# Local projections of a transformer block: q and k as fp32r products, rows turned a tile earlier, q and k rotated together

## The reference

```python
DIM, DEPTH, HEADS, DIM_HEAD, WINDOW, INNER = 256, 2, 8, 64, 128, 512
def _layer(x, wqkv, qs, ksc, wo, ...):
    b, n, _ = x.shape
    h = shift_token(x)              # second half of the features comes from the token before
    qkv = h @ wqkv                  # 256 -> 3 x 512
    q, k, v = jnp.split(qkv, 3, axis=-1)
    q, k, v = (to_heads(q), to_heads(k), to_heads(v))
    q = l2norm(q) * qs
    k = l2norm(k) * ksc
    q, k = rotary_xpos(q, k)        # q*cos*scale + rotate_half(q)*sin*scale; k likewise with 1/scale
    o = local_attention(q, k, v)    # windows of 128, each with the one before
    x = x + o @ wo
    ...
```

## Time and profile before

| | |
|---|---|
| median of 3 runs | 2562.07 us (2554.25 to 2565.87) |
| the profiled execution | 2577.46 us |
| its span, first to last instruction | 2575.8 us |
| busy: TensorE | 2240.0 us (87%) |
| busy: VectorE | 1242.6 us (48%) |
| busy: ScalarE | 1043.7 us (41%) |
| busy: GpSimd | 691.2 us (27%) |
| mean granted TensorE clock | 0.946 |
| first stage of local projections | from 542.5 to 674.6 us |
| second stage | from 937.3 to 1067.9 us |

### The profile page before, as it was taken

The page is one execution under the profiler, slowest core; times in us unless marked ns, Lnnn a source line. Parts: engine busy times, 40 slices in busy tenths (PEclk is TensorE's granted clock), DMA queues, the critical chain, the costliest instruction groups (busy, mean ns, idle before and its releaser), DMA issues. The chain is left out here.

```text
span 2575.8 us, 43116 instructions
## 1 busy us (share of the span) xinstructions
PE 2240.0 (87%) x13642; PEld 1649.2 (64%) x13643; DVE 1242.6 (48%) x2758; ACT 1043.7 (41%) x2555; POOL 691.2 (27%) x684
## 2 busy tenths in 40 slices
PE   7997497769897999898998989799998489879998
PEld 4664497534565864466875654479997256557887
DVE  4664200479775249876325653000000456567864
ACT  1663132313565433466424652124443046544332
POOL 1000201347422547522531001300001410054443
PEclk8998699889999999999999999899999689999999
DMA  7761242110000000000028622113221376100000
GB/s 190 160 156 69 82 166 83 31 41 0 25 0 16 24 17 0 25 0 15 1 47 146 125 36 86 51 47 128 83 105 46 102 149 128 33 27 25 25 25 33
DMA packets 110695, 164.17 MB, mean 64 GB/s; under 512 B 15258, under 2 KB 95115, under 8 KB 105579
## 3 DMA queue, kind: packets, MB, share of 16 engines
q1 hardware_dynamic: 101570, 140.55, 21.6%
q0 software_dynamic: 7680, 20.98, 2.6%
q10 hardware_dynamic: 1320, 1.03, 0.2%
HBM read 114.83 MB, written 47.32 MB: 63 GB/s over the span
## 5 line engine op out<-in xcount | busy, mean ns | idle before, releaser
L1037 DVE TENSOR_REDUCE xa_mx<-ps 128x2 f32<-128x512 f32 x384 | 246.8, 685 | 98.3 <-PE ps L689 97.2
L141 PE MATMUL ps<-ones 128*128 128x384 f32 (+1 forms) x450 | 163.9, 493 | 100.2 <-DMA ex_rows<-rows_out,rows_back 37.8
L896 ACT ACTIVATE xn_tok<-ps 128x512 f32<-128x512 f32 x384 | 210.5, 602 | 52.6 <-PE ps L697 50.9
L1467 PEld LDWEIGHTS ps<-ex_xT,ex_w 128*128 128x128 f32 x1792 | 211.8, 194 | 7.3 <-issue 4.5
L1467 PE MATMUL ps<-ex_xT,ex_w 128*128 128x128 f32 x1792 | 212.4, 277 | 3.8 <-issue 3.8
L1474 PE MATMUL ps<-ex_w,ex_h 128*128 128x256 f32 x896 | 202.7, 379 | 0.0
L141 PEld LDWEIGHTS ps<-ones 128*128 128x128 f32 x450 | 90.3, 221 | 144.7 <-issue 51.6
L689 PE MATMUL ps<-xa_ks,xa_qs 48*128 48x256 f32 (+1 forms) x768 | 158.5, 324 | 27.0 <-DMA xa_qs<-x_queries 8.9
L1474 PEld LDWEIGHTS ps<-ex_w,ex_h 128*128 128x128 f32 x896 | 165.9, 190 | 20.2
L2128 PE MATMUL ps<-lo_w,lp_hs 128*128 128x512 f32 x384 | 173.6, 603 | 4.7 <-ACT lp_hs L2176 2.8
L689 PEld LDWEIGHTS ps<-xa_ks,xa_qs 48*128 48x128 f32 (+1 forms) x768 | 107.7, 194 | 100.3 <-DVE xa_mx L1037 51.2
(11 more groups left out here) (345 smaller groups left out, 4994.9 us busy)
## 6 DMA issues: line engine op xcount, KB each, us to landing
xa_ks<-x_keys SPq DMA_DIRECT2D x144, 128.0 KB
xa_qs<-x_queries SPq DMA_DIRECT2D x144, 128.0 KB, 4.5
ex_w<-in_L0f_w_dram SPq DMA_DIRECT2D x16, 1024.0 KB, 7.2
ex_w<-in_L2f_w_dram SPq DMA_DIRECT2D x16, 1024.0 KB, 6.8
x_keys<-xa_khl SPq DMA_DIRECT2D x24, 512.0 KB, 5.6
x_queries<-xa_qhl SPq DMA_DIRECT2D x24, 512.0 KB, 3.0
ex_stage<-rows_in POOLq DMA_DIRECT2D x64, 128.0 KB
rows_out<-ex_rows SPq DMA_DIRECT2D x56, 128.0 KB, 1.7
```

The source lines that it names most:

```text
L141: self.nc.tensor.matmul(self.ps[:, bank, 0:wide * P], self.ones[:], self.ones[:].unsqueeze(1).to_broadcast([P, wide, P]), start=True, stop ...
L896: nc.scalar.activation(pT[:, h % SLOTS].rearrange("p k q -> p (k q)"), c.ps[:, S_BANK + (HEADS * b + n) % 3], ACT.Exp).then_inc(exped.sem, 1)
L1037: nc.vector.tensor_reduce(mx[:, half, :, col], c.ps[:, M_BANK + h % 2].rearrange("p (t n) -> p t n", t=2), AX_X, ALU.max).then_inc(max_put ...
L1467: ins = nc.tensor.matmul(c.ps[:, f % 4, 0:P], w1[:, buf, k, f * P:(f + 1) * P], xT[:, k], start=(k == 0), stop=(k == KD - 1))
```

## The change

Four things in `local_projections`, and what goes with them:

- q and k are made of fp32r products. Weights and rows are split into a rounded part (`lead`) and the rest (`less`). A tile's list on TensorE is: rounded rows times rounded weights and times the rests of the weights (8 products), v as before (2 fp32 products), then the rests of the rows times the rounded weights (4 products). ScalarE copies the turned rows twice, first rounded, then whole; GpSimd subtracts (`rest`). At the start of a layer ScalarE rounds the weights of q and k, and VectorE subtracts.
- `turn_rows(i + 1, ...)` stands ahead of `project(i, 1)` in TensorE's loop, with the same wait. On ScalarE the copies of the rows stand ahead of the square.
- VectorE rotates q and k of a tile together, with four operations of twice the size; GpSimd rotates nothing.
- `wo` is loaded at the start of `local_weighing` instead of during the projections; squares and t2 share a buffer; four `keep_busy` products stand behind the first `turn_rows`.

The diff, cut:

```diff
 def rotate
+        def rotate(dve, step, tt):
+            a = t1[:, tt].rearrange("p a (h d) -> p a h d", h=LH)
+            b = t2.rearrange("p a (h d) -> p a h d", h=LH)
             for lo, hi in ((0, HALF), (HALF, LD)):
...
+                step.mark(nc.vector.tensor_tensor(
+                    b[:, :, :, lo:hi], src, tab[:, :, 1, tt, lo:hi].unsqueeze(2).to_broadcast([P, 2, LH, HALF]), ALU.mult))
+            step.settle(dve)
+            step.link(dve, nc.vector.tensor_tensor(
+                a, a, tab[:, :, 0, tt].unsqueeze(2).to_broadcast([P, 2, LH, LD]), ALU.mult))
+            return nc.vector.tensor_tensor(a, a, b, ALU.add)
@@ gpsimd
-            def rotate_k(i, tt):
...
+            def rest(i):
+                pool.wait_ge(*h_put(i + 1))
+                nc.gpsimd.tensor_tensor(hl[:], hs[:], hh[:].bitcast(F32), ALU.subtract).then_inc(h_rest.sem, 1)
             stage(0)
+            rest(0)
             with pool.Fori(0, B - 1) as i:
                 stage(i + 1)
-                rotate_k(i, 0)
-                rotate_k(i, 1)
+                rest(i + 1)
@@ tensor, project(i, tt)
-                pe.wait_ge(*h_put(i + 1))
+                pe.wait_ge(*h_lead(i + 1))
                 pe.wait_ge(*lengthed(2 * i + max(tt - 1, 0)) if tt else lengthed(2 * i - 1))
                 pe.wait_ge(*v_put(2 * i) if tt else v_put(2 * i - 1))
-                for n in range(3):
+                rows = slice(tt * P, (tt + 1) * P)
+                for n in range(2):
+                    pe.wait_ge(*w_rest(n + 1))
+                    for a, wp in enumerate((wh, wl)):
+                        for k in range(KD):
+                            nc.tensor.matmul(c.ps[:, 3 * tt + n, :], hh[:, k, rows], wp[:, k, n * INNER:(n + 1) * INNER],
+                                             start=(a == 0 and k == 0), stop=False)
+                pe.wait_ge(*h_put(i + 1))
+                for k in range(KD):
+                    nc.tensor.matmul(c.ps[:, 3 * tt + 2, :], hs[:, k, rows], wqkv[:, k, 2 * INNER:], start=(k == 0),
+                                     stop=(k == KD - 1))
+                pe.wait_ge(*h_rest(i + 1))
+                for n in range(2):
                     for k in range(KD):
-                        ins = nc.tensor.matmul(c.ps[:, 3 * tt + n, :], hs[:, k, tt * P:(tt + 1) * P],
-                                               wqkv[:, k, n * INNER:(n + 1) * INNER],
-                                               start=(k == 0), stop=(k == KD - 1))
+                        ins = nc.tensor.matmul(c.ps[:, 3 * tt + n, :], hl[:, k, rows], wh[:, k, n * INNER:(n + 1) * INNER],
+                                               start=False, stop=(k == KD - 1))
@@ tensor, the list
             turn_rows(0, h_put(0))
-            pe.wait_ge(*w_in(16))
+            c.keep_busy(4, 0)
+            pe.wait_ge(*pool_s(2))
...
                 project(i, 0)
                 turn_qk(i - 1, 0, i + 1)
+                turn_rows(i + 1, qk_put(4 * i - 2))
                 project(i, 1)
-                turn_rows(i + 1, qk_put(4 * i - 2))
                 turn_qk(i - 1, 1, i + 2)
@@ scalar
-                nc.scalar.copy(hs[:, 0, :], c.ps[:, 6, 0:S])
-                nc.scalar.copy(hs[:, 1, 1:S], c.ps[:, 6, S:2 * S - 1]).then_inc(h_put.sem, 1)
+                for rows, sgn in ((hh, h_lead), (hs, h_put)):
+                    nc.scalar.copy(rows[:, 0, :], c.ps[:, 6, 0:S])
+                    nc.scalar.copy(rows[:, 1, 1:S], c.ps[:, 6, S:2 * S - 1]).then_inc(sgn.sem, 1)
             def take(i, tt, between=None):
                 act.wait_ge(*qkv_done(2 * i + tt + 1))
+                if between is not None:
+                    put_rows(between)
                 act.wait_ge(*summed(2 * i + tt))
                 nc.scalar.activation(sq, ..., ACT.Square).then_inc(squared.sem, 1)
-                if between is not None:
-                    put_rows(between)
...
+            act.wait_ge(*w_in(16))
+            lead_w(0)
             put_rows(0)
+            lead_w(1)
@@ vector
+            for n in range(2):
+                cols = slice(n * INNER, (n + 1) * INNER)
+                dve.wait_ge(*w_lead(n + 1))
+                nc.vector.tensor_tensor(wl[:, :, cols], wqkv[:, :, cols], wh[:, :, cols].bitcast(F32), ALU.subtract
+                                        ).then_inc(w_rest.sem, 1)
@@ local_weighing
+            sp.wait_ge(*loaded(16))
+            sp.dma_start(wo[:], dram["L1f_wo"][d]).then_inc(loaded.sem, 16)
```

More of the change, by code:

```diff
@@ L2063, in local_projections @@
         zst, hs = sb("zst", [P, 2, D]), sb("hs", [P, KD, S])
-        sq, ss = sb("sq", [P, 2 * INNER]), sb("ss", [P, 2, 2 * LH])
+        (wh, wl), (hh, hl) = ([c.sb(f"lp_{n}_{part}", shape, F32R, ctx) for part in ("lead", "less")]
+                              for n, shape in (("w", [P, KD, 2 * INNER]), ("h", [P, KD, S])))
+        w_lead, w_rest, h_lead, h_rest = (c.sig(n) for n in ("w_lead_put", "w_rest_put", "h_lead_put", "h_rest_put"))
+        ss = sb("ss", [P, 2, 2 * LH])
         root, rn = sb("root", [P, 2, 2 * LH]), sb("rn", [P, 2, 2 * LH])
@@ L2073, in _ @@
             fetch(sp)
-        def rotate(engine, eng, step, tt, side):
-            a = t1[:, tt, side].rearrange("p (h d) -> p h d", h=LH)
-            b = t2[:, tt, side].rearrange("p (h d) -> p h d", h=LH)
+        def rotate(dve, step, tt):
+            a = t1[:, tt].rearrange("p a (h d) -> p a h d", h=LH)
+            b = t2.rearrange("p a (h d) -> p a h d", h=LH)
             for lo, hi in ((0, HALF), (HALF, LD)):
[L2080 to L2086, removed]
+                src = a[:, :, :, HALF - lo:HALF - lo + HALF]
+                step.mark(nc.vector.tensor_tensor(
[4 more added lines that the diff above has]
+            return nc.vector.tensor_tensor(a, a, b, ALU.add)
         @block.gpsimd
@@ L2090, in _ @@
             nc.gpsimd.memset(hs[:, 1, 0:1], 0.0).then_inc(pool_s.sem, 1)
+            pool.wait_ge(*pool_s(1))
+            nc.gpsimd.tensor_copy(hh[:, 1, 0:1], hs[:, 1, 0:1]).then_inc(pool_s.sem, 1)
             def stage(i):
@@ L2193, in put_qk, with lead_w @@
                                    c.ps[:, 7 - side, :].rearrange("p (h t) -> p h t", h=HC)).then_inc(qk_put.sem, 1)
+            def lead_w(n):
+                cols = slice(n * INNER, (n + 1) * INNER)
+                nc.scalar.copy(wh[:, :, cols], wqkv[:, :, cols]).then_inc(w_lead.sem, 1)
+            act.wait_ge(*w_in(16))
+            lead_w(0)
             put_rows(0)
+            lead_w(1)
             take(0, 0)
@@ L2227, in _ @@
                     dve.wait_ge(*squared(2 * i + tt + 1))
-                    nc.vector.tensor_reduce(ss[:, tt], sq[:].rearrange("p (h d) -> p h d", d=LD), AX_X, ALU.add
+                    nc.vector.tensor_reduce(ss[:, tt], sq.rearrange("p (h d) -> p h d", d=LD), AX_X, ALU.add
                                             ).then_inc(summed.sem, 1)
@@ L2240, in _ @@
                     rot.n = SETUP + 3 * tt
-                    rotate(nc.vector, dve, rot, tt, 0).then_inc(q_rot.sem, 1)
+                    rotate(dve, rot, tt).then_inc(qk_rot.sem, 1)
     loaded.spent(32)
-    pool_s.spent(1 + 6 * B)
+    pool_s.spent(2)
+    for sgn in (w_lead, w_rest):
+        sgn.spent(2)
+    for sgn in (h_lead, h_rest):
+        sgn.spent(B)
     pair_s.spent(SETUP + 6 * B)
@@ L2337, in output @@
             def output(i):
+                pe.wait_ge(*loaded(32))
                 pe.wait_ge(*o_put(2 * i + 2))
@@ L2491, in local_attention @@
         v = c.sb("la_v", [P, NT, INNER], ctx=ctx)
-        wo, mask = c.sb("la_wo", [P, INNER // P, D], ctx=ctx), c.sb("la_mask", [P, 3 * WIN], ctx=ctx)
+        mask = c.sb("la_mask", [P, 3 * WIN], ctx=ctx)
         def fetch(sp):
-            sp.dma_start(wo[:], c.dram["L1f_wo"][d]).then_inc(c.sig("output_weights_in").sem, 16)
             sp.dma_start(mask[:], c.dram["window"]).then_inc(c.sig("output_weights_in").sem, 16)
-        t1, t2 = (c.xT[:, k].rearrange("p (t a n) -> p t a n", t=2, a=2) for k in range(KD))
-        local_projections(c, d, z, qT, kT, v, t1, t2, w, w_in, fetch)
+        t1 = c.xT[:, 0].rearrange("p (t a n) -> p t a n", t=2, a=2)
+        t2, sq = c.xT[:, 1, 0:2 * INNER].rearrange("p (a n) -> p a n", a=2), c.xT[:, 1, 2 * INNER:4 * INNER]
+        local_projections(c, d, z, qT, kT, v, t1, t2, sq, w, w_in, fetch)
         w_in.spent(16)
-        local_weighing(c, d, z, zstats, qT, kT, v, wo, mask, w, w_in)
+        local_weighing(c, d, z, zstats, qT, kT, v, mask, w, w_in)
 def local_ff(c, d, z, zstats, w1, w1_in, last):
```

31 lines of the change are left out of this document (13 added, 18 removed).

## The result

The change is slower: 2616.8 us (median of 4 runs, 2616.3 to 2620.1) against 2564.0 (4 runs, 2554.3 to 2572.4; the 2562.1 from which the prediction starts is the median of three of them), a ratio of 1.021 with a 95% interval of 1.018 to 1.023. That is +52.8 us, where +45.6 was forecast.

The account below looks back on a forecast made before the run. VectorE (92.5 of 100 us) and TensorE (91.3) were taken as close to full. Ring 27.5 + clock fall 19.8 - start and end 1.7 = +45.6 us on 2562.1, forecasting 2607.7 us, range 2582 to 2634.

Parts of the forecast that it names:

- The order: Loop: turn_rows ahead makes project(i, 1) wait for VectorE's reduction through ScalarE's root and copies; +2.29 us a round, +27.5 us.
- The ring without the clock: Loop round closed through VectorE's reduction, ScalarE's root and copies, turn_rows, project(i, 1) and square: 17.12 us instead of 14.83.
- TensorE's wait: Ahead of turn_rows in each round: TensorE idle for 4.5 us, where its longest wait was 1.08.
- The clock: Behind TensorE's wait in each round: granted clock falls, costing 1.65 us a round, +19.8 us; bounds 0 and 4.5 a round.
- The clock did not hold: Rival, TensorE in the loop: same ring without a clock fall, +25.8 us, 2587.9 us; chance 0.18.
- it did not stay low for all of project(i, 1): Rival, TensorE in the loop: low clock throughout project(i, 1), 12 x 4.5 us, +79.8, 2642 us; chance 0.07.
- The wait of turn_rows is not hidden: Rival, TensorE's loop: wait hidden, VectorE sets rounds of 14.4 us, 2555.6 us, chance 0.07; with faster rotation 2540, chance 0.02.
- the fp32r products are cheap: Rival, TensorE's projections: fp32r products cost 0.44 us each, half of fp32 ones, 12 x 2.5 more, 2638 us; chance 0.02.
- The products: TensorE's projection with 12 fp32r products for q and k: 4.63 us instead of 5.41, 0.227 each.
- The rotation: VectorE rotating q and k together: 3.83 us a tile instead of 4.02 for q alone, which GpSimd held up.
- GpSimd's subtraction costed at nothing: Loop: GpSimd's subtraction and row copy fall in VectorE's idle time, cost nothing; without that cover at most 1.29 + 0.61 a round.
- Start and end: Outside the loops: starts +1.6 and +1.1, three tiles of each layer -1.6, ends -1.4 twice; together -1.7 us.

Follow-up runs that it names:

- experiment 2: The change with six unused filler products in TensorE's wait ahead of turn_rows(i+1), against the kernel before: 2590.0 us, ratio 1.009, rounds 17.15 us.
- Experiment 1: The change with turn_rows(i+1) put back behind project(i, 1), all else kept, against the kernel before: 2568.7 us, ratio 0.999.
- experiment 6: The change with ScalarE's copies of turned q and k ahead of its root in a round's first tile, against the kernel before: 2563.1 us, ratio 0.997.
- experiment 4: The kernel before with only turn_rows(i+1) moved ahead of project(i, 1), against the kernel before: 2612.0 us, ratio 1.016.
- experiment 5: The change with fp32 products and two row copies, its order and joint rotation kept, against the kernel before: 2607.2 us, ratio 1.017.
- experiment 8: The kernel before with only the joint rotation of q and k on VectorE, GpSimd just copying rows, against the kernel before: 2552.1 us, ratio 0.9955.
- experiment 7: The change with ScalarE's copies of turned q and k ahead of the root in both tiles, against the kernel before: 2567.9 us, ratio 1.001.
- experiment 3: The change with three unused filler products in TensorE's wait ahead of turn_rows(i+1), against the kernel before: 2595.2 us, ratio 1.012.

## Why the prediction was right, point by point

- *The order.* Right in mechanism, place and size. The ring without the clock was put at 17.12 us and is 17.15 (experiment 2); that it is so close has some luck in it, as the way from the reduction of the first tile to that of the second is 10.07 us (put: 9.96) and the way back 7.08 (put: 7.16). TensorE's wait was put at 4.5 us and is 4.2. Its links were the ones named: the wait for turned k, the root ahead of its copy, the square behind four row copies. Experiment 1 takes the order away, 6 the link on ScalarE, 4 puts the order alone on the old kernel; the loss goes and comes with them.
- *The clock.* The mechanism was right, the size off: 1.65 us a round was put in as the mean of two other places (1.9 and 1.5, whose mean is 1.7); it is 2.17. This one term, 12 x 0.52 = 6.2 us, is most of the 7.2 us by which the forecast increase is low (of the 9.1 us between 2607.7 and 2616.8 the other 1.9 are the base, 2562.1 against 2564.0). The term is mis-sized because a wait's price was taken from waits that came once: the loss differs from round to round. From turn_rows to the end of the projection the first three rounds took 7.7 (569.86 to 577.60), 6.4 and 7.3 us against 4.97 in experiment 2 (610.61 to 615.58): 2.8, 1.4 and 2.3 lost, 2.2 in the mean.
- *The rivals.* The clock did not hold, and it did not stay low for all of project(i, 1): the dearest rounds lost 2.8 us, where all of it would be 4.5. The wait of turn_rows is not hidden (4.2 us), and the fp32r products are cheap.
- *The products.* A projection without a wait and at full clock is 4.55 us (598.52 to 603.07), put at 4.47 without its tail. Right. In project(i+1, 0) it was worth nothing, as TensorE had 4.2 us to spare; in project(i, 1), which is on the ring, the 0.78 us saved were for the most part given back to the two further row copies (0.54): experiment 5's ring is 0.1 us longer.
- *The rotation.* 3.74 us measured, put at 3.83, because two operations of 512 elements take 1.29 us together and not 2 x 0.69, the second starting before the record of the first ends. That q alone took 4.02 on account of GpSimd is shown by experiment 8: twice the work takes 3.73 us in the tile beside which GpSimd does nothing, and 4.14 in the one on which its copy falls (583.31 to 587.45).
- *GpSimd's subtraction costed at nothing.* Right here, if not quite by the cover that was named: the subtraction lay in VectorE's idle time, the copy beside a reduction that was not held up by it. Where the two fall on rotations, in experiments 1 and 7, a round is 1.3 and 1.1 us longer than twice the undisturbed 7.07; at most 1.9 had been put.
- *Start and end.* The first reduction comes 0.7 and 1.6 us later in its stage (put: 1.6 and 1.1). The fillers, put at 4.7 us at the low level, took 3.4, since the clock rose earlier than thought:

```profile
542.69 3.90 PE L141 MATMUL ps<-ones 128*128 128x384 f32 x8
...
545.10 1.46 DVE L2235 TENSOR_TENSOR lp_w_less<-lo_w,lp_w_lead 128x1024 fp32r<-128x1024 f32 x1 [1.97 <-ACT lp_w_lead L2210]
...
546.13 0.92 PE L2132 MATMUL ps<-lp_w_lead,lp_h_lead 128*128 128x512 f32 x2
...
551.12 1.03 ACT L2196 ACTIVATE xn_T<-ps 128x1024 f32<-128x1024 f32 x1 [6.05 <-PE ps L2141]
...
552.18 1.22 DVE L2253 TENSOR_REDUCE lp_ss<-xn_T 128x16 f32<-128x1024 f32 x1 [4.25 <-ACT xn_T L2196]
```

  In the second tile two operations of GpSimd fell on the rotation (8.05 us between the first two reductions), which was not put in. The end is 1.7 us shorter in each layer, put at 1.4 and 0.2 for the last tile. The sum was -1.7 and is -0.3.

## What to carry to other kernels

A step that is moved ahead in one engine's list brings its wait along: before moving it, follow that wait back through the queue of the engine that serves it, and see what stands ahead there. If the answer is something that depends on the work now behind the moved step, two loose engines become one ring, and no engine's busy share shows it. A wait of some us on TensorE, returning in each round, then costs more than its own length: here 2.2 of the 4.5 us a round were the clock, and six useless products took them away.

Where VectorE's two-input operations run beside GpSimd's, giving GpSimd's share to VectorE can be faster; look at the durations of the same shape with and without GpSimd beside them.

## What the runs showed of the hardware that I had not expected

- The clock's answer to a wait of TensorE in this stage, in the rounds behind the first of each layer: after 2.2 us no fall in any of ten (experiment 3), after 2.88 us a fall in all five of one layer and in none of the other (4), after 3.6 us in all ten (5), after 4.2 us in all ten (the change). The length alone does not decide: besides the two layers of experiment 4, in experiment 6 one turning of the first layer's six was slow behind 1.7 us.
- The fall comes within the wait, so that the work behind it starts at 1.2 GHz (the change: 0.77 granted in the wait, each turn_rows 1.11 or 1.12 us), or only in the work behind it (experiments 4 and 5; the wait of 2.86 us in the earlier trace rows has 1.00 itself, and the 3.4 us behind it 0.56). So the duration of the first instruction behind a wait does not tell whether the wait cost clock; the granted clock of the next some us does.
- GpSimd's operations are held up by VectorE's too. Its copy of the rows takes 0.61 us beside VectorE's reduction and 1.61 beside its rotation (604.68 in experiment 7).
